# Expert stages of a fused MoE and attention block: weight splits, part and evacuation reordered, a second item transposed on TensorE

## The reference, cut to what matters

```python
cap = int(s * F_C / e)                                    # 256
scores = softmax(hidden @ gate_w.T, axis=-1).transpose(0, 2, 1)
topk_w, topk_idx = top_k(scores, cap)
x_tok = take_along_axis(hidden[:, None], topk_idx[..., None], axis=2)
g = einsum('becd,efd->becf', x_tok, Wg)
u = einsum('becd,efd->becf', x_tok, Wu)
h = gelu(g, approximate=False) * u
eo = einsum('becf,edf->becd', h, Wd) * topk_w[..., None]
flat = flat.at[flat_idx].add(eo)                          # scatter-add of the rows
out = flat + shared_expert(hidden)
x = x + 0.5 * ffn(norm(x)); x = x + attention(norm(x)); x = x + 0.5 * ffn(norm(x))
```

## Time and profile before

| what | value |
|---|---|
| median of 3 runs | 1556.11 us |
| the profiled execution's own time | 1550.99 us |
| span of its trace | 1549.3 us |
| PE busy | 1470.5 us (95%) |
| ACT busy | 1090.0 us (70%) |
| DVE busy | 894.1 us (58%) |
| POOL busy | 557.6 us (36%) |
| DMA | 196.77 MB, mean 127 GB/s |
| mean granted TensorE clock | 0.990 |
| routed items of the first FFN | about 186 to 478 us |
| attention with its projections | about 490 to 1088 us |
| routed items of the second FFN | about 1251 to 1546 us |

### The profile page before, as it was taken

The page is one execution under the profiler, slowest core; times in us unless marked ns, Lnnn a source line. Parts: engine busy times, 40 slices in busy tenths (PEclk is TensorE's granted clock), DMA queues, the critical chain, the costliest instruction groups (busy, mean ns, idle before and its releaser), DMA issues. The chain is left out here.

```text
span 1549.3 us, 26559 instructions
## 1 busy us (share of the span) xinstructions
PE 1470.5 (95%) x9841; PEld 1020.2 (66%) x9845; DVE 894.1 (58%) x1982; ACT 1090.0 (70%) x1395; POOL 557.6 (36%) x500
## 2 busy tenths in 40 slices
PE   5999989999889999999999999999999989999997
PEld 4788878888788773333343343343788878888887
DVE  7888656666656882231145152036888856666664
ACT  7322366767654889999999999999622357767672
POOL 5000435566635981211121121120200145566654
PEclk9999999999999999999999999999999999999999
DMA  8212467777746689515246063222412266678763
GB/s 295 75 55 69 120 175 174 174 185 184 188 91 144 221 272 219 92 19 84 38 89 137 29 125 55 30 69 78 134 55 69 71 178 165 165 182 186 180 167 41
DMA packets 184561, 196.77 MB, mean 127 GB/s; under 512 B 81456, under 2 KB 146480, under 8 KB 181680
## 3 DMA queue, kind: packets, MB, share of 16 engines
q1 hardware_dynamic: 156256, 147.35, 36.8%
q0 software_dynamic: 28176, 47.73, 14.6%
HBM read 123.73 MB, written 55.57 MB: 116 GB/s over the span
## 5 line engine op out<-in xcount | busy, mean ns | idle before, releaser
L2483 ACT ACTIVATE 6345_pr<-6345_pS 128x1024 f32<-128x1024 f32 x448 | 420.5, 1190 | 2.3 <-PE 6345_pS L2375 2.2
L2406 PE MATMUL 6345_pO<-6345_pr,6330_vres 128*32 128x512 f32 x1792 | 237.8, 604 | 0.7 <-ACT 6345_pr L2483 0.7
L2375 PEld LDWEIGHTS 6345_pS<-sq_rows,sk_rows 50*128 50x128 f32 x896 | 77.4, 184 | 179.6 <-ACT 6345_pr L2483 131.9
L2375 PE MATMUL 6345_pS<-sq_rows,sk_rows 50*128 50x512 f32 x896 | 183.6, 468 | 2.6 <-issue 1.3
L351 PE MATMUL 6356_pGU<-columns_ahead,weights_wts 128*128 128x512 f32 (+1 forms) x400 | 158.3, 396 | 17.0 <-ACT 6356_gl L1091 13.6
L351 PE MATMUL 93_pGU<-columns_ahead,weights_wts 128*128 128x512 f32 (+1 forms) x368 | 146.0, 397 | 20.3 <-ACT 93_gl L1091 18.1
L1095 ACT ACTIVATE hidden_hT<-6356_hf 128x512 fp32r<-128x512 f32 (+1 forms) x100 | 61.5, 615 | 131.2 <-DVE 6356_hf L1275 129.7
L1095 ACT ACTIVATE hidden_hT<-93_hf 128x512 fp32r<-128x512 f32 x96 | 60.7, 632 | 132.1 <-DVE 93_hf L1275 132.1
L352 PE MATMUL 6356_pGU<-columns_ahead,weights_wts 128*128 128x512 f32 (+1 forms) x400 | 153.5, 384 | 0.0
L353 PE MATMUL 6356_pGU<-columns_ahead,weights_wts 128*128 128x512 f32 (+1 forms) x400 | 153.3, 383 | 0.0
L2507 POOL TENSOR_SCALAR_AFFINE_SELECT 6345_pr<-6345_pr 128x512 f32<-128x512 f32 x32 | 20.5, 641 | 358.1 <-ACT 6345_pr L2483 358.1
(11 more groups left out here) (437 smaller groups left out, 3596.7 us busy)
## 6 DMA issues: line engine op xcount, KB each, us to landing
93_raw_g<-WgT SPq DMA_DIRECT2D x16, 512.0 KB
...
6356_raw_g<-WgT SPq DMA_DIRECT2D x16, 512.0 KB
6356_raw_u<-WuT SPq DMA_DIRECT2D x16, 512.0 KB
6356_raw_d<-WdT SPq DMA_DIRECT2D x16, 512.0 KB
```

The lines of the kernel that those rows point to most:

```text
L2375: m = t_.matmul(to[:, e, :], key, query, start=True, stop=True)
L2406: m = t_.matmul(pO[e * 32:(e + 1) * 32, j % 2, off:off + wd], vres[:, (g // GB) * TPB + kt, at:at + 32], from_(e), start=n == first[j], st ...
L2483: s_exp.done(a.activation(to, pS[:, u % RING, :, :], ACT.Exp, scale=HD ** -0.5))
```

## The change

All edits are in `ffn`:
- ACT, stages 9 to 23: `hidden` is cut in `gelu` and `high`. The splits of weights 0 and 1 move from ahead of quarter 0 to between the GELU and the high half of quarters 0 and 1. `part_planes(s + 1)` moves from ahead of `split(s, 2)` and quarter 2's GELU to behind that GELU. The splits that the first FFN does for its last items keep their places around `join_planes`.
- DVE, stages 9 to 23: `split(s, 0)` stands behind `mul(s, 0)`, and `split(s, 1)` between `mul(s, 1)` and `low(s, 1)`; the first half of `evacuate` stands ahead of `lower`, the second behind it; each `low` follows its `mul` more closely. In `last_steps` the split of weight 1 stands ahead of `lower`.
- Item 9 (`BY_PE`), like item 8, is turned by PE: eight transposes between `gu(9, 1)` and `gu(9, 2)`, and `gathered` in place of `join_planes` and `lower`. Its turn waits until DVE has emptied the two banks of item 8.
- The numbers of `part_planes`, `turn_planes` and `join_planes` start one item later.
- SP: `turn_planes(item)` is issued behind the expert's three weight loads and no longer between the second and the third.
- POOL: `gather` of item 11 waits for PE's turn of item 9; the wait for parted planes starts one item later.

```diff
--- before.py
+++ after.py
@@ -454,6 +454,7 @@
         nc, ALU, ACT, AX, bass = self.nc, self.ALU, self.ACT, self.AX, self.bass
         f32, f32r, bf16 = self.f32, self.f32r, self.bf16
         J, NI, W = NQ, NQ + E, 4 * P
+        BY_PE = J + 1
         KN = 6
         with self.scope() as t:
             KB = 1024
@@ -767,8 +768,8 @@
                     s_res[d % 2].done(sp.dma_start(eo[:, d % 2, :, :], xv[d]))
 
                 def turn_planes(item):
-                    s_planes.wait(sp, item - J)
-                    s_joined.wait(sp, DC * (item - J - 1))
+                    s_planes.wait(sp, item - BY_PE)
+                    s_joined.wait(sp, DC * (item - BY_PE - 1))
                     s_planes_turned.done(sp.dma_start_transpose(turned_planes[:, :, :, :, :].rearrange("p q h c t -> p (q h c) t"),
                                                                 planes[:, :, :].rearrange("p q w -> p (q w)")))
 
@@ -803,12 +804,10 @@
                 load_residual(7)
                 load_weight(1, 1)
                 load_weight(1, 2)
-                turn_planes(J + 1)
                 for e in range(2, E):
-                    load_weight(e, 0)
-                    load_weight(e, 1)
+                    for w in range(3):
+                        load_weight(e, w)
                     turn_planes(J + e)
-                    load_weight(e, 2)
                 if lead:
                     self.load_projection_weights(sp)
                     s_wl.wait(sp, 3 * E)
@@ -968,6 +967,8 @@
                 def turn(item, c):
                     if c == 0:
                         s_rows[item % 2].wait(t_, (item - J) // 2 + 1)
+                    if item > J:
+                        s_xl.wait(t_, lowered(item - 1) + c + 1)
                     for q in range(4):
                         m = t_.transpose(turned(c)[:, q * P:(q + 1) * P], xr[:, item % 2, q, c * P:(c + 1) * P], self.ident[:, :])
                     s_T.done(m)
@@ -1011,6 +1012,9 @@
                             down(s, 0)
                             down(s, 1)
                         gu(s, 1)
+                    if s == BY_PE:
+                        turn(s, 0)
+                        turn(s, 1)
                     if s > NI:
                         last_down(NI - 1)
                     elif s > J + 1 and not (lead and s == NI):
@@ -1053,12 +1057,12 @@
 
                 def part_planes(item):
                     s_rows[item % 2].wait(a, (item - J) // 2 + 1)
-                    s_planes_turned.wait(a, item - J - 1)
+                    s_planes_turned.wait(a, item - BY_PE - 1)
                     halves = xr[:, item % 2, :, 0:D].bitcast(self.u16).rearrange("p q (d h) -> p q h d", h=2)
                     s_planes.done(a.activation(planes[:, :, :].rearrange("p q (h d) -> p q h d", h=2), halves, ACT.Copy))
 
                 def join_planes(item):
-                    n, col = item - J, column(item)
+                    n, col = item - BY_PE, column(item)
                     s_planes_turned.wait(a, n)
                     s_U.wait(a, 4 * (item - 1))
                     for c in range(DC):
@@ -1084,11 +1088,18 @@
                     s_ex.done(a.activation(ex[:, tiles, :], dif[:, tiles, :], ACT.Exp))
 
                 def hidden(s, f, h=None):
-                    i = s - 1
+                    gelu(s, f, h)
+                    high(s, f, h)
+
+                def gelu(s, f, h=None):
                     n, cut = number(s, f, h), piece_of(h)
                     a.wait_ge(*s_G.at(n + 1))
                     s_mul.wait(a, n - 1)
                     s_gelu.done(a.activation(gl[:, f % 2, cut], pG(f % 2)[:, cut], ACT.Gelu))
+
+                def high(s, f, h=None):
+                    i = s - 1
+                    n, cut = number(s, f, h), piece_of(h)
                     a.wait_ge(*s_mul.at(n + 1))
                     if f == 0:
                         s_D.wait(a, 2 * (i - 1))
@@ -1142,11 +1153,37 @@
                         continue
                     if s == J + 1:
                         gathered(J)
-                    if s == J + 1:
-                        part_planes(s)
-                    if J < s < NI - (2 if lead else 0):
-                        split(s, 0)
-                        split(s, 1)
+                    if J < s < NI:
+                        own_weights = s < NI - (2 if lead else 0)
+                        gelu(s, 0)
+                        if own_weights:
+                            split(s, 0)
+                        high(s, 0)
+                        gelu(s, 1)
+                        if own_weights:
+                            split(s, 1)
+                        high(s, 1)
+                        if lead and s == NI - 2:
+                            split(s, 2)
+                            split(s + 1, 0)
+                        if s == BY_PE:
+                            gathered(s)
+                        else:
+                            join_planes(s)
+                        if own_weights:
+                            split(s, 2)
+                        if lead and s == NI - 3:
+                            split(s + 1, 0)
+                            split(s + 1, 1)
+                        if lead and s == NI - 2:
+                            split(s + 1, 1)
+                            split(s + 1, 2)
+                        gelu(s, 2)
+                        if s < NI - 1:
+                            part_planes(s + 1)
+                        high(s, 2)
+                        hidden(s, 3)
+                        continue
                     hidden(s, 0)
                     if lead and s == NI:
                         s_D.wait(a, 2 * (NI - 3))
@@ -1154,23 +1191,8 @@
                         self.counter("proj_w", 16).wait(a, 2)
                         s_wh.done(a.activation(self.lead_w[0][:, :, :], self.qkv_raw[:, :, :], ACT.Copy))
                     hidden(s, 1)
-                    if lead and s == NI - 2:
-                        split(s, 2)
-                        split(s + 1, 0)
                     if J - 3 <= s < J:
                         split(J, s - J + 3)
-                    if J < s < NI:
-                        join_planes(s)
-                    if J < s < NI - 1:
-                        part_planes(s + 1)
-                    if J < s < NI - (2 if lead else 0):
-                        split(s, 2)
-                    if lead and s == NI - 3:
-                        split(s + 1, 0)
-                        split(s + 1, 1)
-                    if lead and s == NI - 2:
-                        split(s + 1, 1)
-                        split(s + 1, 2)
                     hidden(s, 2)
                     hidden(s, 3)
                 if lead:
@@ -1393,9 +1415,9 @@
                     if s == NI - 2:
                         split(s + 1, 0)
                     if s < NI:
-                        lower(s)
                         if s < NI - 1:
                             split(s if s == NI - 3 else s + 1, 1)
+                        lower(s)
                         evacuate(s, 0)
                         evacuate(s, 1)
                         gate_weights(s)
@@ -1493,30 +1515,32 @@
                         if s == NI:
                             last_item(s)
                         continue
+                    mul(s, 0)
                     split(s, 0)
-                    mul(s, 0)
+                    low(s, 0)
                     mul(s, 1)
-                    low(s, 0)
+                    split(s, 1)
                     low(s, 1)
-                    lower(s)
-                    split(s, 1)
-                    if s > J + 1:
+                    if s == BY_PE:
+                        gathered(s)
+                    else:
                         evacuate(s, 0)
+                        lower(s)
                         evacuate(s, 1)
                     gate_weights(s)
                     split(s, 2)
                     mul(s, 2)
+                    low(s, 2)
                     mul(s, 3)
-                    low(s, 2)
                     low(s, 3)
 
             def on_gpsimd(g):
                 def gather(item):
                     k, e = item % 2, item - J
                     if e >= 2:
-                        if e == 2:
-                            s_T.wait(g, DC)
-                        s_planes.wait(g, e - 2)
+                        if item - 2 <= BY_PE:
+                            s_T.wait(g, DC * (e - 1))
+                        s_planes.wait(g, item - 2 - BY_PE)
                         s_wt.wait(g, e - 1)
                     self.settle(g)
                     for q in range(4):
```

## The result

The changed kernel takes 1496.54 us (median of 4 runs, 1496.14 to 1497.23), the kernel before beside it 1556.08 us (4 runs, 1554.93 to 1557.19): a ratio of 0.9618 [0.9601, 0.9635]. The profiled execution of after took 1497.23 us (span 1495.5 us), that of before 1550.99 us: 53.8 us apart.

What follows compares the result with a forecast made beforehand. PE, busy 95% of the span, was taken to bound the kernel; 27.7 (steady) + 10.5 (item 9) + 8.0 (ends) + 2.2 (clock) - 4 (hand-offs) = 44.4, say 45 us off 1556.1, gave 1511 us, range 1502 to 1530.

Steps and rivals of the forecast that it cites:

- the offset of 5.1 us: Whole program: the runs' median lies 5.1 us above the profiled execution, so the forecast was taken from 1556.1 us.
- the hand-off charge of 4 us: Routed stages: new hand-offs charged at 0.15 us for each of 27 stages, 4 us lost.
- The steady stall: 25 routed stages: parting ahead of quarter 2's GELU on ACT makes PE stall; moving it gains 27.7 us.
- Earlier evacuation: cost nothing: DVE's earlier evacuation lets POOL scatter some 3 us earlier, covered by POOL's and DMA's idle time; cost nothing.
- Item 9 by PE: Stage 9 of each FFN: PE's transposes replace the DMA's stalls of 5.94 and 6.12 us at 0.8 us each; gain 10.5 us.
- that wait is covered: SP's queue: the transposing DMA waits behind load 2 for DVE's split 2 (13.7), but planes are parted only at 15.3.
- The ends: First FFN, stages 21 and 22: stalls of 6.01 and 4.56 us shrink, gaining 8.0 us, plus 2.2 us of slow clock.
- 1: Steady stages: planes become a loop through the transposing DMA; at 10.5 us a stage lasts 17.3, total 1526; chance 0.12.
- 2: Steady stages: same planes loop, slower; at 12.6 us for the DMA a stage lasts 19.4, total 1578; chance 0.04.
- 3: Stalls of stages 21 and 22 shrink only by half and PE's turn costs 3.0 us; total 1520; chance 0.09.
- 4: Behind item 9's turn by PE the granted clock falls, costing 4 us; total 1515; chance 0.03.
- 5: Whole change: it moves waits without effect; total 1556; chance 0.02.

Runs made afterwards that it cites:

- before_third: The kernel before, unchanged, measured a third time: 1555.9 us.
- evac_only: The kernel before with only the first half of DVE's evacuation moved ahead of `lower`: 1530.26 us.
- partsp_back: Changed kernel with parting back ahead of split 2 and quarter 2's GELU, and SP's transposing DMA back between loads 1 and 2: 1508.61 us.
- splits_part_sp_back: Changed kernel with the splits of weights 0 and 1, the parting and SP's order all put back: 1509.6 us.
- evac_back: Changed kernel with only DVE's evacuation put back, both halves behind `lower`: 1500.67 us.
- turn_back: Changed kernel with only item 9's turn put back to planes and a transposing DMA: 1516.1 us.
- part_back: Changed kernel with only the parting put back ahead of split 2 and quarter 2's GELU, SP's order staying new: 1523.05 us.
- three_back: Changed kernel with splits, parting and evacuation all put back; item 9's turn, SP's order and `last_steps` stay new: 1554.4 us.
- splits_back: Changed kernel with only ACT's and DVE's splits of weights 0 and 1 put back: 1525.87 us.
- splits_only: The kernel before with only ACT's and DVE's splits of weights 0 and 1 moved as in the change: 1545.92 us.
- part_only: The kernel before with only the parting behind quarter 2's GELU and SP's transposing DMA behind the three loads: 1549.4 us.
- turn_only: The kernel before with only item 9 turned by PE: 1542.89 us.
- run 7: Changed kernel with item 9's turn put back (1516.1 us), and repeats of the changed kernel (1497.58 us) and the kernel before (1552.53 us).

## Why the prediction was right or wrong

The direction and most of the size came true, by a cause that was not the one named. The time lies 14.5 us under the forecast and 5.5 us below the range, mostly by four terms: the offset of 5.1 us, the hand-off charge of 4 us, and two pieces left at nothing, the head (2.5 us) and the last item (2.0 us).

- **The steady stall, 27.7 us: the size was right, the cause wrong.** Steady and first together gave 38.6 us against 27.7 + 10.5 = 38.2, because the size of the steady part came from PE's own work, which any cure brings back. How close the sum comes is luck in part: against before_third, with its slow DMA in stage 9, it would have been 45.7 us. The step that failed is the one that put the stall down to the parting ahead of GELU 2. Two chains that close through the evacuation made it. evac_only opens both with the parting in its old place; partsp_back, too, has 16.66 us with the old place. The change held two cures, the evacuation and the pair of splits and late parting. What the pair brings beside the evacuation is at the ends and in the firsts (splits_part_sp_back).
- **"Earlier evacuation: cost nothing" failed.** It was costed as a cover for scatters, and alone it is worth 26.7 us (23.5 of them steady, against before_third). It looks free only in the presence of the other cure (evac_back).
- **Item 9 by PE: 10.5 us plus the slow clock behind it, which I had put with the steady stages.** Measured 14.3 us on the first traces, 16.8 in turn_back. The 0.79 us of the turn and the clock were right. What I missed is that the removed DMA's 8.28 us was one draw of 8.1 to 11.9 us.
- **SP: "that wait is covered", right for PE in the changed kernel, but with no room for more.** The joining waits for the transposing DMA in six stages, up to 3.10 us, and PE loses nothing. With the splits, the parting or all three parts back, the new SP order costs time in the steady stages (part_back, three_back, and splits_back by its rows). At the ends it does what was forecast: ACT's wait of 4.85 us in stage 22 is gone, and comes back as 5.10 us in partsp_back.
- **The ends: 10.2 us, measured 11.4.** 8.6 us are idle time of PE (forecast 8.0), the rest mostly the slow clock behind it (forecast 2.2). Left over 1.33 and 0.68 us against 1.7 and 0.9, and their causes (the low half of a weight on DVE, `mul` 2) are those named.
- **The hand-off charge of 4 us failed.** The steady stages last what PE's work lasts. Hand-offs lie on the other engines, which have 3 us in hand.
- **The last item, left at nothing: 2.0 us.** splits_only and evac_only have it too, part_only and turn_only do not, so it seems to hang on when the last item's chain starts; this was not followed further. The text allowed for it only in the lower end of the range.
- **The head: 2.5 us that no part explains**; it comes and goes with the execution (run 7), and the kernel before has it as well (7.48 in before_third).
- **The offset of 5.1 us failed.** I moved the profiled execution's sum to the level of the runs. But before's level is made by its wait for the transposing DMA in stage 9: 60.97 us in the firsts at 1550.99 us, 68.96 in the execution of before_third that took 1556.2, with a head of 2.5 us less. The changed kernel does not wait there, and its medians are 1496.54 and 1497.58 us. Without the offset the forecast would have been 1506 us.

Summed on the traces: 44.4 us forecast, and 4 (hand-offs) + 2.5 (head) + 2.0 (last) + 1.2 (ends) + 0.4 (first and steady) - 0.7 (elsewhere) more make 53.8. With the 5.1 us of offset that is the whole miss of some 14.5 us.

**The rivals.** 1 did not decide the changed kernel, but its loop is real. The transposing DMA reached the joining late five times in the first FFN of after, once 10.0 us behind its issue (262.32 to 272.32), and once in the second FFN 10.99 us behind it (1247.64 to 1258.63), where the prediction set the limit at 9.9; never twice far enough to reach PE. The limit itself was set too high: a late joining is followed by the next issue after 7.3 us or more and not 6.8, which leaves 9.3 us. In splits_back this loop, through split 2 and load 2, closes at 8.2 us and costs PE 15.9 us in the steady stages. 2 did not come. It drew on the Trainium skill, "DMA: Bandwidth & Descriptors", on queues, rings and completion order, by which a transpose starts behind the load ahead of it: with the same load 0.4 us ahead the DMA took 8.28 and 11.88 us, so that order alone does not set the time. What did hold a transpose back is SP's own queue (part_back), where it stands behind a load that waits. 3 did not come. 4 did not come: behind both turns the granted clock is 1.00, so the rule in the Trainium skill, "TensorE: Matmul & The Clock Gate", on PE-mode transpose shows no effect for eight transposes between dense matmuls. 5 did not come.
